# Second halves of q and k projected one pair later, silu's table loaded ahead of v's copy, and a reordered prologue

## The reference, cut to what matters

```python
x = x + L0(_gn(x))   # group norm over 4 channels, then a mixture of convolutions
x = x + L1(_gn(x))   # group norm over 4 channels, then window attention
# L0: shared 1x1 convolution and the 2 of 8 expert 3x3 convolutions that a router picks per image,
#     each in 8 groups, group norm over 16 channels, gamma and beta, silu; weighted sum
shared = silu(group_norm(conv1x1(x)))
expert_out = (silu(group_norm(conv3x3_of_the_2_experts(x))) * rw).sum(axis=1)
# L1: 16 windows of 8x8 pixels per image, 8 heads of 16 channels
q, k, v = qkv_w @ x + qkv_b
attn = softmax(q @ k.T / 4 + bias)
out = proj_w @ (window_reverse(attn @ v) + depthwise7x7(v)) + proj_b
```

## Time and profile before

| what | value |
|---|---|
| median of 3 executions | 714.65 us |
| the profiled execution's own time | 716.12 us |
| its span, first to last instruction | 714.4 us |
| PE busy | 594.1 us (83%) |
| DVE busy | 535.4 us (75%) |
| ACT busy | 453.3 us (63%) |
| POOL busy | 371.6 us (52%) |
| mean granted TensorE clock | 0.951 |

### The profile page before, as it was taken

One profiled execution on the slowest core, in us unless ns is written; L12 is line 12 of the kernel. 1 busy time (PEld: TensorE's weight loads), 2 busy tenths in 40 slices (PEclk: granted clock), 3 DMA queues, 4 the chain that ended last, 5 costly groups with the idle time before them and its releaser, 6 DMA issues.

```text
span 714.4 us, 19187 instructions
## 1 busy us (share of the span) xinstructions
PE 594.1 (83%) x6958; PEld 354.3 (50%) x6958; DVE 535.4 (75%) x967; ACT 453.3 (63%) x761; POOL 371.6 (52%) x599
## 2 busy tenths in 40 slices
PE   4417468898989898998989898998989898989891
PEld 3401133546556564655556564655656676544330
DVE  3862456698888988887988988888898878323791
ACT  2213375778677878778687877878687754446450
POOL 5145655766566766747666766756662201000282
PEclk9997575999999999999999999999999899999997
DMA  8822244647584655758484665758563344473294
GB/s 319 317 80 91 86 153 116 200 138 226 157 231 139 195 184 146 231 157 220 140 229 148 185 184 157 227 158 236 148 173 116 93 136 130 151 260 103 58 249 165
DMA packets 57603, 122.06 MB, mean 171 GB/s; under 512 B 12195, under 2 KB 29990, under 8 KB 57510
## 3 DMA queue, kind: packets, MB, share of 16 engines
q1 hardware_dynamic: 42982, 80.35, 36.7%
q0 software_dynamic: 13664, 37.35, 18.7%
q10 hardware_dynamic: 864, 3.15, 1.3%
HBM read 70.59 MB, written 41.81 MB: 157 GB/s over the span
## 4 chain that ended last, share of the span: by engine, by line
PE 48%; ACT 18%; issue 12%; DVE 9%; POOL 5%; DMA 4%; POOLq 2%; SPq 0%; DVEq 0%; ACTq 0%
PE g L1207 7%; PE g L1187 6%; ACT y L652 5%; PE pv L1272 5%; PE t L1257 5%; PE g L1391 4%; ACT vp L698 4%; DMA vt<-x 4%; PE g L1217 4%; PE s L1246 3%; PE t L1312 3%; PE g L1189 2%; PE g L1282 2%; PE s L1312 2%; PE s L1242 2%
## 5 line engine op out<-in xcount | busy, mean ns | idle before, releaser
L1000 DVE TENSOR_REDUCE mx<-s 128x8 f32<-128x512 f32 x128 | 86.9, 679 | 26.8 <-PE s L1246 26.6
L647 ACT ACTIVATE y<-g 128x512 f32<-128x512 f32 x96 | 55.7, 600 | 74.0 <-PE g L1189 62.9
L1257 PE MATMUL t<-ident,less 128*128 128x128 f32 x512 | 79.5, 279 | 15.5 <-ACT pt L719 15.5
L1004 DVE TENSOR_TENSOR less<-s,mx 128x512 f32<-128x512 f32 x128 | 88.5, 691 | 4.4
L1257 PEld LDWEIGHTS t<-ident,less 128*128 128x128 f32 x512 | 62.5, 146 | 44.2 <-issue 36.6
L1272 PE MATMUL pv<-vp,pt 128*64 128x34 f32 x2048 | 79.5, 222 | 5.2 <-DVE ot L1018 5.0
L719 ACT ACTIVATE pt<-t 128x512 f32<-128x512 f32 x128 | 74.8, 597 | 12.0 <-PE t L1257 10.8
L1187 PE MATMUL g<-xa,wsa 128*128 128x512 f16 x192 | 59.0, 420 | 27.0 <-DMA xb<-xs 14.9
L954 DVE BATCH_NORM_STATS2 st<-y 128x6 f32<-128x512 f32 x96 | 63.1, 684 | 23.6 <-ACT y L647 23.3
L1272 PEld LDWEIGHTS pv<-vp,pt 128*64 128x64 f32 x2048 | 71.4, 139 | 7.5 <-issue 3.8
L1207 PE MATMUL g<-xw,w 128*128 128x512 f32 x128 | 67.2, 649 | 2.5 <-ACT y L647 0.9
(11 more groups left out here) (179 smaller groups left out, 1302.3 us busy)
## 6 DMA issues: line engine op xcount, KB each, us to landing
xs<-xhl POOLq DMA_DIRECT2D x16, 578.0 KB, 3.5
vt<-x SPq DMA_DIRECT2D x4, 2048.0 KB, 17.5
xin<-x POOLq DMA_DIRECT2D x16, 512.0 KB, 6.8
sq_d<-qhl SPq DMA_DIRECT2D x32, 256.0 KB, 2.2
sk_d<-khl SPq DMA_DIRECT2D x32, 256.0 KB, 2.8
stack<-sk_d SPq DMA_DIRECT2D x64, 128.0 KB, 3.6
stack<-sq_d SPq DMA_DIRECT2D x64, 128.0 KB, 3.7
vt<-vst SPq DMA_DIRECT2D x128, 64.0 KB, 3.1
```

Source lines behind the costliest of these rows:

```text
L1000: v.tensor_reduce(mx[:, p % 2, :], scored, AX.X, ALU.max).then_inc(sem["s_max"], 1)
L1004: v.tensor_tensor(less[:, p % 2, :].rearrange("p (h m) -> p h m", h=HEADS), scored, mx[:, p % 2, :].unsqueeze(2).to_broadcast([C, HEADS, T ...
L1257: last = nc.tensor.transpose(tbk[p % 2][:, C * i:C * i + C], less[:, p % 2, C * i:C * i + C], ident[:, :])
```

## The change

- The second halves of q and k (project_qk, high_qk, low_qk for h = 1) go from pair 1 of the turn to pair 2, on PE behind average and turn_outputs, on ACT behind turn_out, on DVE behind the maxima of pair 2. bank_uses follows.
- ACT gets one more activation: Silu of one column (warm) in pair 3, after that pair's exponential and ahead of v_out. The instruction that loads silu's table goes with the first Silu after an Exp, so it stands ahead of v's copy.
- In the prologue, average(0, 1) goes ahead of convolve(1, 1), average(1, 1) ahead of the first scores; group_means(0, 1) ahead of y_stats(1, 0), group_means(1, 1) ahead of the first maxima; on POOL, the loads for image 1 are spread around y_affine(0) and x_affine(0).

```diff
--- before.py
+++ after.py
@@ -97,9 +97,12 @@
     for b in range(B + 1):
         for h in range(2):
             use("y2", b + 2, (h,))
-            use("q", b + 1, (h,))
-            use("k", b + 1, (h,))
+            if h == 0:
+                use("q", b + 1, (0,))
+                use("k", b + 1, (0,))
         use("ot", b - 1, (1,))
+        use("q", b + 1, (1,))
+        use("k", b + 1, (1,))
         use("v", b + 1)
         use("pr", b - 1)
         use("vt", b + 1)
@@ -199,6 +202,7 @@
         coef = sb("coef", [C, 2, 3])
         shift = sb("shift", [C, 3])
         coef2 = sb("coef2", [C, 2])
+        warm = sb("warm", [C, 1])
         mx = sb("mx", [C, 2, HEADS])
         btot = sb("btot", [C, 1])
         sst = sb("sst", [C, 2 * B, 6])
@@ -566,13 +570,14 @@
             choose_affine(0)
             form_xn(1)
             save_xn(1)
+            load_weights(1, 0)
             y_affine(0)
-            for k in range(TOP):
-                load_weights(1, k)
-                load_rows(1, k)
+            load_rows(1, 0)
+            load_weights(1, 1)
+            x_affine(0)
+            load_rows(1, 1)
             choose_affine(1)
             load_x(2)
-            x_affine(0)
             form_xn(2)
             save_xn(2)
             y_affine(1)
@@ -751,12 +756,18 @@
                             copy_y(b + 2, 2, (p,))
                         if has3 and p == 0:
                             high_xn(b + 3)
+                        if has1 and p == 0:
+                            high_qk(b + 1, 0, 0)
+                            high_qk(b + 1, 1, 0)
+                    if p == 2:
+                        if b:
+                            turn_out(b - 1, 1)
                         if has1:
-                            high_qk(b + 1, 0, p)
-                            high_qk(b + 1, 1, p)
-                    if p == 2 and b:
-                        turn_out(b - 1, 1)
+                            high_qk(b + 1, 0, 1)
+                            high_qk(b + 1, 1, 1)
                     if p == 3:
+                        if has2:
+                            act.activation(warm[:, :], power[:, 0:1], ACT.Silu)
                         if has1:
                             v_out(b + 1)
                         if has2:
@@ -1065,9 +1076,12 @@
                     if p < 2:
                         if has2:
                             y_stats(b + 2, 2, (p,))
-                        if has1:
-                            low_qk(b + 1, 0, p)
-                            low_qk(b + 1, 1, p)
+                        if has1 and p == 0:
+                            low_qk(b + 1, 0, 0)
+                            low_qk(b + 1, 1, 0)
+                    if p == 2 and has1:
+                        low_qk(b + 1, 0, 1)
+                        low_qk(b + 1, 1, 1)
                     if p == 4:
                         if b:
                             add_projection(b - 1, 0)
@@ -1093,8 +1107,8 @@
             group_means(0, 0)
             for part in range(3):
                 residual(0, part)
+            group_means(0, 1)
             y_stats(1, 0)
-            group_means(0, 1)
             y_stats(1, 1)
             y_stats(1, 2)
             for n in range(2):
@@ -1103,9 +1117,9 @@
             group_means(1, 0)
             for part in range(3):
                 residual(1, part)
+            group_means(1, 1)
             maxima(0, 0)
             y_stats(2, 0)
-            group_means(1, 1)
             maxima(0, 1)
             y_stats(2, 1)
             turn_v(0)
@@ -1326,14 +1340,17 @@
                     if p < 2:
                         if has2:
                             convolve(b + 2, 2, (p,))
-                        if has1:
-                            project_qk(b + 1, 0, p)
-                            project_qk(b + 1, 1, p)
+                        if has1 and p == 0:
+                            project_qk(b + 1, 0, 0)
+                            project_qk(b + 1, 1, 0)
                     if p == 2:
                         if has2:
                             average(b + 2, 0, 3, AV16)
                         if b:
                             turn_outputs(b - 1, 1)
+                        if has1:
+                            project_qk(b + 1, 0, 1)
+                            project_qk(b + 1, 1, 1)
                     if p == 3 and has1:
                         project_v(b + 1)
                     if p == 4 and b:
@@ -1356,8 +1373,8 @@
                 convolve(0, k)
             convolve(1, 0)
             average(0, 0, 3, AV16)
+            average(0, 1, 1, AV4)
             convolve(1, 1)
-            average(0, 1, 1, AV4)
             convolve(1, 2)
             for n in range(2):
                 for h in range(2):
@@ -1366,8 +1383,8 @@
             project_v(0)
             project_vt(0)
             convolve(2, 0)
+            average(1, 1, 1, AV4)
             scores(0, 0)
-            average(1, 1, 1, AV4)
             scores(0, 1)
             convolve(2, 1)
             images(step)
```

## The result

The changed kernel takes **735.16 us** (median of 4 runs, 732.66 to 736.07), the kernel before, beside it, 715.28 (4 runs). The ratio is 1.0246, 95% interval 1.0211 to 1.0281: slower. 729.5 had been forecast, range 713 to 738. The profiled execution took 736.07 with a span of 734.4, against 716.12 and 714.4 before: 20.0 us more of span.

What follows compares the result with a forecast made beforehand. Two equally long chains, ACT's with silu's table load and DVE's with POOL's, were taken to bound the kernel. Span 714.4 + 13.0 (loop) + 1.8 (prologue) = 729.2, corrected and rounded to 729.5 us; range 713 to 738.

Steps and rivals of the forecast that it cites:

- PE waits 1.30 us at average: On PE in pair 2, average comes 1.82 us sooner but its sums do not, so it waits 1.30 us each turn.
- The ring: Loop from average through q, k, gs, coef, POOL's sum and DVE back to average: 32.88 us against 31.70, +1.18 a turn.
- gs waited for nothing of q and k before: On DVE, gs now stands behind low_qk and so behind average; before, it was said to wait for none of these.
- Eleven turns: Of 13 intervals between images 2 and 15, 11 were taken to pay 1.18 us each: +13.0 us.
- the image that was late before: An image whose coef came late already had more than 1.18 us of waiting and was to cost nothing more.
- the first comes out of the prologue, where POOL is behind anyway: Reason for leaving the first of the 13 intervals out of the turns that pay 1.18 us.
- silu's load, gain 0: ACT's table load is hidden before v's copy, but silu then waits for coef: gain 0; without the ring up to 1.28 us a turn.
- The stacks, cost 0: First-half stacks of q and k on SP land later, but slack covers it: cost 0.
- the 0.7 us of slack: What was taken to be left of 3.1 us spare between the stacks' landing and PE's need for them.
- The prologue, +1.8 us: The reordered prologue was to cost +1.8 us, bounds -2 and +3.
- the late convolution: In the prologue, convolve(1,2) waits for later row DMAs and starts near 89.3 instead of 86.27: 3.0 us late.

Runs made afterwards that it cites:

- gs first: The changed kernel with DVE's group_means(b+2, 0) in pair 2, right behind the maxima and ahead of low_qk: 730.73 us, ratio 1.0203, period 32.56 us.
- q and k alone: The kernel before with only the second halves of q and k moved to pair 2, no warm activation, old prologue: 736.52 us, ratio 1.0238.
- the stacks sooner: The changed kernel with SP issuing the first half's stacks before saving the second halves of q and k: 738.29 us, ratio 1.0308.
- the silu load alone: The kernel before with only the warm activation ahead of v_out: 711.09 us, ratio 0.990; again 709.93 us, ratio 0.9907.
- gs first with stacks sooner: The changed kernel with gs copied ahead of the low halves and SP's first-half stacks issued before the second halves are saved: 729.04 us, ratio 1.0179.
- the silu load and the changed prologue: The kernel before with the warm activation and the new prologue, q and k not moved: 713.65 us, ratio 0.9966, and 713.25, ratio 0.9949.

## Why the prediction was right, and where it was off

- **PE waits 1.30 us at average: there, but smaller, and split as said.** 0.63 at average and 0.33 one step before, 0.96 together. 1.04 us more stands at the earlier values matmul, which the forecast did not have; DVE starts its run on POOL's sum there, after a wait of 0.36 us.
- **The ring, 32.88 us: right.** Each of its seven terms came within 0.05 us, the sum is 32.92. What the forecast lacked is the second ring through average, which the run with gs first shows at 32.56; alone it would cost 0.86 us a turn. The sentence that gs waited for nothing of q and k before goes too far: the low half of k stood between the sums and gs already (417.78 in the earlier trace rows). New are its place behind average and behind the maxima, 0.93 and 0.80 us.
- **Eleven turns: the images 4 to 15 right, image 3 wrong.** The images 4 to 15, without the image that was late before, brought what 11 turns should: 14.8 us, of which 1.6 are the clock's in image 12, against 13.0. But "the first comes out of the prologue, where POOL is behind anyway" failed: image 3's interval grew by 3.07 us. It is no accident of one run: 31.1 or 31.2 in the two kernels with the loop of before without the silu load, 34.2, 33.8 and 33.3 in the changed kernel, in q and k alone, and with the stacks sooner. The ring bound there before (28.61 + 2.57 = 31.18, measured 31.16) and binds now: gs comes 4.29 us behind the sums instead of 2.57, 1.7 us of the 3.07. In the other 1.35 us the sums come later. The run with the stacks sooner takes 1.0 off by removing one stack wait; the remainder goes with a longer stretch at the lower clock (last section). PE's other wait there, for an exponential, is not new: 1.66 us, and 2.59 before. These parts are read from single profiles.
- **silu's load, gain 0: right here.** Its cover is gs's lateness, as said. The changed kernel against q and k alone is 32.91 against 33.08 us a turn, so up to 0.17 us a turn is gained after all; the two ratios, 1.0246 and 1.0238, show none of it. Without the q and k move it gains 0.52 us a turn, 1.0% in all.
- **The stacks, cost 0: right for the ordinary turn, though the 0.7 us of slack was not there.** PE waits for them in about half of the turns, 5.7 us in sum. With q and k alone there are only 0.6 us of such waits and the period is no shorter, and taking the waits away shows no gain in time in either of two kernels. About 1 us was paid once, in image 3's interval.
- **The prologue, +1.8 us: the late convolution as forecast, its cost only on the average.** Measured from image 0's coef, convolve(1,2) starts 86.95 - 71.76 = 15.19 us behind it, before 86.27 - 74.18 = 12.09: 3.1 us late, forecast 3.0. It is 15.1 to 15.3 in all eight profiles with the new prologue and 12.1 to 12.2 in the five with the old. It waits for its rows, 3.30 us where the earlier trace rows had 0.41. On the clock of the span it stands at 86.95 and not at 89.3, because image 0's coef came 2.4 us sooner in this execution; the forecast took it as fixed, and that the profile then shows only +0.10 at image 1's coef is luck. What the late start costs varies: from image 0's coef to image 1's it is 29.8 to 30.0 us in six of the eight and 31.5 in two, against 29.2 to 29.3 in four of the five and 27.44 in the profile of the earlier trace rows alone. On the average image 1's coef starts at 102.79 with the new prologue (100.71 to 104.81) and at 101.27 with the old one (100.50 to 102.40): +1.5. The two comparisons of times give 0.9 to 4.9 and 3.3 us.

PE in the timeline of the changed kernel's prologue:

```profile
79.74 1.44 PE L1201 MATMUL g<-xa,wsa 128*128 128x512 f16 x3
...
86.95 1.46 PE L1201 MATMUL g<-xa,wsa 128*128 128x512 f16 x3 [3.30 <-DMA xb<-xs]
```

- **What the sum left out.** 20.0 us came where 14.8 were forecast: prologue -1.7, image 3 +3.1, image 12 +1.6 (the clock, below), the tail +2.0, rounding the rest. So the median of 735.16 lies 5.7 us above the forecast, near the upper end of its range, for reasons that the sum did not hold. The tail's part is not settled: from image 15's coef to the end, two runs of the same kernel, with the silu load alone, took 164.1 and 170.4 us.

No kernel run here beats the one with the silu load alone, 1.0% and 0.9% below the kernel before in its two runs.

## What to carry to other kernels

Before work is moved to the front of a queue, look at what it covered: matmuls that seem to stand in the way may be the ones behind which the next operand becomes ready. Write the rings out, from one event to the same event a turn later, across all engines; the longest ring is the period, and the others tell what a gain on it can bring (here 0.52 us where silu came 1.4 us sooner). A wait that newly shows, like the one for the stacks, says nothing until a kernel without it has been timed. And a time that is read off two profiles is best measured from the same event in both: from the span's start the late convolution of the prologue seemed 0.7 us late, from image 0's coef it is 3.1.

## What the runs showed of the hardware

TensorE's clock can fall in the middle of the steady loop. PE in the timeline of the changed kernel at image 12, and the busy time by stretches (stretch, us, busy of PE, PEld, DVE, ACT, POOL, granted clock, DMA share, GB/s):

```profile
451.32 0.66 PE L1286 MATMUL pv<-vp,pt 128*64 128x34 f32 x16 [1.34 <-DVE ot L1029]
...
452.98 3.67 PE L1221 MATMUL g<-xw,w 128*128 128x512 f32 x4
```

```profile
448.00:451.00 3.00, 1.98 (x19) 1.27 (x18) 2.93 (x5) 2.37 (x5) 2.52 (x5) 1.00 0.76 167
451.50:456.50 5.00, 5.00 (x25) 2.00 (x23) 3.58 (x6) 3.24 (x6) 3.84 (x3) 0.66 0.01 3
```

Before the fall PE had waited 1.34 us, after waits of 0.52 and 0.83 us in the 9 us ahead of it. The granted clock is 0.66 on average over the second stretch and 0.50 from 454 to 456, which is the lower level, 1.2 GHz instead of 2.4. The q matmuls take 3.67 us there instead of 1.98, and this turn 34.55 us instead of 32.91. With the stacks sooner the same happened behind a wait of 1.66 us, in a turn of 36.2 us, and with gs ahead of the low halves twice, behind stack waits of 1.54 and 1.49 us, in turns of 33.6 us. So a wait can cost more than itself.

The length of the wait does not decide it alone. In the changed kernel one of 1.35 us at 352.0 brought no fall, nor did 1.36 in the kernel before. At the start of image 3's interval nearly the same wait was followed by three different stretches (the kernel before, stacks sooner, gs first with stacks sooner; PE in the timeline, then the stretch 142 to 150 of each):

```profile
141.69 0.63 PE L1257 MATMUL t<-ident,less 128*128 128x128 f32 x4 [2.59 <-ACT pt L719]
...
143.16 1.08 PE L1274 MATMUL t<-ident,less 128*128 128x128 f32 x4 [2.60 <-ACT pt L727]
...
143.09 0.63 PE L1274 MATMUL t<-ident,less 128*128 128x128 f32 x4 [2.59 <-ACT pt L727]
```

```profile
142.00:150.00 8.00, 7.96 (x73) 4.15 (x71) 7.72 (x13) 5.89 (x13) 4.34 (x14) 0.79 0.84 226
142.00:150.00 8.00, 6.84 (x39) 3.35 (x39) 6.17 (x10) 6.25 (x14) 5.39 (x12) 0.57 0.92 232
142.00:150.00 8.00, 5.54 (x52) 2.85 (x54) 5.98 (x10) 6.84 (x16) 5.59 (x12) 1.00 0.81 213
```

The mean clocks 0.79, 0.57 and 1.00 are about 3.4, 6.8 and 0 us at the lower level. The changed kernel and q and k alone have the 6.8 us there, and so has one of the two runs of the kernel with the silu load and the changed prologue: its interval is 31.53 us, and 31.16 in the other, with 3.4 us. So the longer stretch costs some 0.4 us of the 3.07 in image 3. What makes the clock fall in one execution and not in the other is open.
